# Three layers of gated attention: part of L1's and L2's softmax on GpSimd, another order of steps, and fillers in L2

## The chip, the cores and the metric

The kernel runs as one program on one NeuronCore of a Trainium2 chip. The metric is the device time of that core in microseconds (us). TensorE is called PE in the rows, VectorE DVE, ScalarE ACT, GpSimd POOL, SyncE SP.

## What is computed

The input x is [32, 64, 128] (2,048 tokens of width 128) with a context of [32, 64, 96]. Four layers follow each other; each adds a gated cross attention and a gated feed-forward block:

```python
x = x + tanh(g_xattn[n]) * xattn_n(layernorm(x), ctx)
x = x + tanh(g_ffn[n]) * ffn_n(layernorm(x))
```

The change touches the attentions of layers 1 and 2, "L1" and "L2" below. Both are ordinary multi-head attentions inside each of the 32 batches (64 queries by 64 keys), all in f32:

```python
attn = einsum("bqhd,bkhd->bhqk", Q, K) * scale      # L1: 8 heads of 16; L2: 16 heads of 8
attn = clip(attn, -10000, 10000)                     # L2 alone
attn = softmax(attn); out = einsum("bhqk,bkhd->bqhd", attn, V) @ W_O
```

## The kernel before

The program is written engine by engine: every engine has its own instruction queue in the order of the source, runs it in that order, and waits on semaphores for the others. Nothing but these written orders and waits sets the order of the work.

**Groups and units.** An attention goes through 8 groups of 4 batches (256 tokens), in a loop whose first and last turns are written out. A group has 4 units, u = 0 to 3. A unit is a quarter of the heads for all 4 batches: a score tile of 128 partitions by 256 columns in L1 and by 512 columns in L2. "Unit u+2" means two units on in this order, across the border of a group too.

**A unit's steps**, with the line of the kernel before:

- PE `scores`: query times key into bank u % 2 of PSUM (L1742)
- DVE `scores`: L2 first clamps the tile into SBUF (L833); then the row maximum (L836) and the subtraction (L838), result in SBUF
- ACT `expo`: exponential in place (L1314)
- DVE `weigh`: row sum (L846), reciprocal (L848), product (L850), which raises `prob`
- PE `turn`: waits for `prob`, transposes the tile in blocks of 128 by 128 into bank 2 + u % 2 (L1762). In L1 it first issues 3 "dense" matmuls whose result nobody reads (L1681; 30 ahead of the first unit)
- ACT `probT`: copies the transposed tile to SBUF (L1318)
- PE `values`: waits for that copy, multiplies with V (L1773)
- ACT `narrow`: copies the result out of PSUM, two copies of 32 partitions by 128 columns (L1369)

**Once a group**: PE `value_rows` (L1719) and `queries_keys` (L1691, L1692), ACT copies of values and queries, DVE `keys`, which spreads the keys by head with a mask (L859 in L2, L864 in L1), PE `project_out` (L1803), DVE `add_group` (L886) and two batch norm statistics (L915). GpSimd makes one copy of the context, 96 by 256, for the next group's values (L487), and nothing else during an attention.

**The written orders before**, one group (numbers are units, a prime marks the next group):

```text
PE : value_rows, scores 2, turn 0, project_out, values 0, turn 1, scores 3, queries_keys',
     values 1, turn 2, scores 0', values 2, turn 3, scores 1', values 3
DVE: weigh 1, scores 2, add_group, weigh 2, scores 3, keys', weigh 3, scores 0', weigh 0', scores 1'
ACT: expo 1, values, probT 0, expo 2, narrow 0, probT 1, queries', expo 3, narrow 1, probT 2,
     expo 0', narrow 2, probT 3, narrow 3
```

L3's attention uses the same functions with orders of its own, which stay.

## Time and profile before

| | us |
|---|---|
| median of 3 runs | 1296.91 (1296.06 to 1301.83) |
| the profiled execution, its own time | 1296.64 |
| its span, first to last instruction | 1294.9 |
| L1 attention, first scores to last project_out | 90.8 |
| L2 attention, the same | 165.3 |
| mean granted TensorE clock | 0.802 of full speed |

The two attentions together are about a fifth of the span. A time inside the span is given from its start. The granted clock has two levels, 2.4 GHz (1.00) and 1.2 GHz (0.50); a figure between them is a mean over a stretch.

### The profile page before, as it was taken

The page shows a single profiled execution, that of the slowest core. Times are in us where ns is not written, and L with a number is a line of the kernel's source. Part 1 is how long each engine was busy: PE and PEld are TensorE (multiplying, and loading weights), DVE is VectorE, ACT ScalarE, POOL GpSimd, SP SyncE. Part 2 cuts the span into 40 slices and gives each one's busy share as a digit, 9 for nine tenths or more (in the row PEclk, how much of TensorE's full clock was granted, in tenths as well). Part 3 has the DMA queues.
Part 4 walks back from the last instruction along what each step waited for, and adds up shares of the span by engine and source line. Part 5 has one row for each costly group of instructions (what it writes and reads, how often), then busy time and mean ns, then how long its engine had stood idle before and what let it go on. Part 6 is the DMA issues. An engine that isn't in the chain of part 4 may idle for free.

```text
span 1294.9 us, 22960 instructions
## 1 busy us (share of the span) xinstructions
PE 896.7 (69%) x7815; PEld 721.9 (56%) x7818; DVE 797.8 (62%) x1904; ACT 477.3 (37%) x1085; POOL 233.0 (18%) x280
## 2 busy tenths in 40 slices
PE   0336335048994783889975779993899999739992
PEld 0216122046763772556653679992677777628771
DVE  3864878966885235888776636555766566462334
ACT  0441308114552452344341343331343344205551
POOL 1000000000000671000000047760000000006771
PEclk9756668567995895677586789995999999659996
DMA  7200000006001118000000101118000000001113
GB/s 190 80 1 1 0 1 0 0 1 147 0 1 33 44 49 234 1 1 0 0 1 0 33 27 47 47 42 213 2 2 0 0 0 0 11 27 45 51 51 109
DMA packets 73143, 48.25 MB, mean 37 GB/s; under 512 B 19642, under 2 KB 65732, under 8 KB 73092
## 3 DMA queue, kind: packets, MB, share of 16 engines
q1 hardware_dynamic: 64484, 31.80, 9.2%
q0 software_dynamic: 6656, 13.64, 3.5%
q10 hardware_dynamic: 1952, 2.15, 0.5%
q8 instruction: 30, 0.49, 0.2%
q14 instruction: 21, 0.17, 0.0%
HBM read 33.93 MB, written 13.63 MB: 37 GB/s over the span
## 4 chain that ended last, share of the span: by engine, by line
PE 47%; DVE 27%; POOL 9%; issue 7%; ACT 6%; DMA 2%; DVEq 0%; SPq 0%; another core or an unknown queue 0%; POOLq 0%; ACTq 0%
PE ps L1909 6%; POOL rows_y L499 4%; POOL arena L494 4%; PE ps L1773 3%; PE ps L1742 3%; PE ps L1803 3%; PE ps L1923 3%; PE ps L1498 3%; PE ps L1762 3%; PE ps L1699 2%; PE ps L1709 2%; PE ps L1787 2%; PE ps L1726 2%; PE ps L1751 2%; DVE bst L523 2%
## 5 line engine op out<-in xcount | busy, mean ns | idle before, releaser
L1909 PE MATMUL ps<-arena 128*128 128x128 f32 x1152 | 153.8, 284 | 0.0
L494 POOL DMA_INDIRECT arena<-rows_x,row_in x104 | 102.8, 988 | 276.7 <-DVEq L1116 245.9
L1909 PEld LDWEIGHTS ps<-arena 128*128 128x128 f32 x1152 | 141.4, 197 | 1.4
L499 POOL DMA_INDIRECT rows_y<-arena,row_out x104 | 108.9, 1047 | 56.4 <-issue 21.3
L1923 PE MATMUL ps<-arena 128*128 x832 | 116.1, 283 | 1.4 <-DVE arena L1079 1.3
L1066 DVE COPY arena<-arena 128x644 f32 (+1 forms) x104 | 61.9, 595 | 78.1 <-DVE arena L1079 31.9
L1923 PEld LDWEIGHTS ps<-arena 128*128 128x128 f32 x832 | 102.1, 193 | 6.0 <-issue 3.3
L1498 PE MATMUL ps<-ident,xh 128*128 128x128 f32 x128 | 36.9, 446 | 85.9 <-DVE xh L555 69.8
L1314 ACT ACTIVATE arena<-arena 128x512 f32<-128x512 f32 (+1 forms) x96 | 53.7, 559 | 111.5 <-DVE arena L838 111.2
L1440 ACT ACTIVATE arena<-ps,arena 128x128 f32<-128x128 f32 x256 | 73.2, 368 | 46.9 <-PE ps L1909 46.9
L1773 PE MATMUL ps<-arena 128*64 128x64 f32 x768 | 71.3, 256 | 19.7 <-ACT arena L1318 16.2
L846 DVE TENSOR_REDUCE arena<-arena 128x8 f32<-128x512 f32 (+1 forms) x96 | 57.1, 595 | 44.1 <-ACT arena L1314 42.8
L1773 PEld LDWEIGHTS ps<-arena 128*64 128x64 f32 x768 | 61.7, 166 | 40.2 <-ACT arena L1318 26.3
L1498 PEld LDWEIGHTS ps<-ident,xh 128*128 128x128 f32 x128 | 22.9, 186 | 99.2 <-DVE xh L555 76.0
L1318 ACT COPY arena<-ps 128x512 f32<-128x512 f32 (+1 forms) x96 | 49.4, 514 | 73.1 <-PE ps L1762 69.4
L1742 PE MATMUL ps<-arena 32*64 32x128 f32 (+1 forms) x512 | 67.7, 401 | 9.1 <-DVE arena L859 6.6
L1079 DVE TENSOR_TENSOR arena<-ps,arena 128x128 f32<-128x128 f32 x64 | 18.7, 292 | 85.6 <-PE ps L1923 85.6
L487 POOL COPY arena<-ctxT 96x256 f32 x16 | 6.9, 429 | 331.2 <-PE ps L1726 168.7
L1762 PE MATMUL ps<-ident,arena 128*128 128x128 f32 x320 | 62.5, 317 | 1.6 <-DVE arena L850 1.4
L1901 PE MATMUL ps<-ident,arena 128*128 128x128 f32 x104 | 32.8, 315 | 41.8 <-DMA arena<-rows_x,row_in 41.0
L850 DVE TENSOR_TENSOR arena<-arena 128x512 f32<-128x512 f32 (+1 forms) x96 | 57.9, 603 | 3.5 <-DVE arena L848 0.2
L1657 PE MATMUL ps<-wffT,arena 128*128 128x128 f32 x96 | 13.9, 319 | 54.1 <-DVE arena L774 54.1
(289 smaller groups left out, 1770.2 us busy)
## 6 DMA issues: line engine op xcount, KB each, us to landing
arena<-rows_y SPq DMA_DIRECT2D x20, 256.0 KB, 4.6
arena<-in_L_ffn_w SPq DMA_DIRECT2D x2, 2048.0 KB, 9.5
arena<-in_L_ffn_w SPq DMA_DIRECT2D x16, 256.0 KB, 6.5
rows_x<-xh SPq DMA_DIRECT2D x3, 1024.0 KB, 5.4
rows_x<-zero SPq DMA_DIRECT2D x1, 2560.0 KB, 9.9
arena<-in_L_ffn_gate_proj SPq DMA_DIRECT2D x8, 256.0 KB, 4.9
arena<-in_L_ffn_up_proj SPq DMA_DIRECT2D x8, 256.0 KB, 4.8
arena<-in_L_ffn_down_proj SPq DMA_DIRECT2D x1, 2048.0 KB, 9.9
```

Of the source, the lines that this page charges most:

```text
L494: g.indirect_dma_start(xq[:, q % 4, :], None, rows_x, bass.IndirectOffsetOnAxis(row_in[:, q:q + 1], 0)).then_inc(sem(f"xq_loaded{q % 4}"), 16)
L499: g.indirect_dma_start(rows_y, bass.IndirectOffsetOnAxis(row_out[:, q:q + 1], 0), yq[:, q % 4, :], None).then_inc(sem(f"y_scattered{q % 4} ...
L846: own(v.tensor_reduce(t["sum"][:, u, 0:n], p_, AX.X, ALU.add))
L850: v.tensor_tensor(p_, p_, t["rec"][:, u, 0:n].unsqueeze(2).to_broadcast([P, n, S]), ALU.mult).then_inc(sem("prob"), 1)
L1066: v.tensor_copy(wst[:, s_ % 4, 0:WS[l]].unsqueeze(1), table(l)[:, bass.ds(e, 1), 0:WS[l]]).then_inc(sem("w_staged"), 1)
L1440: s.activation(hT[:, s_ % 2, f, :], ps[:, s_ % 2, P * f:P * f + P], fn, bias=b1[:, f:f + 1]).then_inc(sem("hidden_ready"), 1)
L1498: ins = pe.transpose(ps[0:w, c % 2, P * k:P * k + P], src[:, j, :], ident[:, :])
L1742: ins = pe.matmul(o.rearrange("p (h c s) -> p h c s", c=2, s=S)[:, :, c, :], t["q"][r:r + 32, 0, lo:lo + S], t["k"][r:r + 32, :, lo:lo + S ...
L1762: ins = pe.transpose(ps[:, 2 + u % 2, P * k:P * k + P], t["p"][:, u, P * k:P * k + P], ident[:, :])
L1773: ins = pe.matmul(ps[0:64, 4 + u % 2, S * hh:S * hh + S], t["v"][:, 4 * hh + u, 64 * k:64 * k + 64], t["pt"][:, u % 2, k, S * hh:S * hh + ...
L1909: ins = pe.matmul(ps[:, 2 * m + s_ % 2, P * f:P * f + P], wst[:, s_ % 4, lo:lo + P], xqT[:, s_ % 2, :], start=True, stop=True)
L1923: ins = pe.matmul(ps[:, 4 + s_ % 2, 0:P], hT[:, s_ % 2, f, :], w2[:, P * f:P * f + P], start=(f == 0), stop=(f == NF - 1))
```

## The change

It does five things to the attentions of L1 and L2.

1. GpSimd gets two new steps for each unit: `total` adds the two halves of each row of exponentials (64 columns to 32) into a new tile `half`, and `weigh` does the product with the reciprocal and raises `prob`. DVE keeps `inverse`: it waits for `half`, sums what is left (half as many columns) and takes the reciprocal.
2. L2 clamps the row maximum (128 by 8) instead of the tile; the lower clamp rides with the subtraction, and one more pass over the tile in SBUF takes the minimum with 0.
3. The orders of DVE, ACT and PE are written anew.
4. `values` writes its two halves to partitions 0 to 63 and 64 to 127 and alternates between them; `narrow` makes four copies of 32 by 64 in place of two.
5. The dense matmuls are issued in L2 as well, 3 before each turn and 30 before the first.

The orders after, one group:

```text
PE  : value_rows, scores 2, turn 0, project_out, values 0, scores 3, turn 1, queries_keys',
      values 1, scores 0', turn 2, values 2, scores 1', turn 3, values 3
DVE : scores 2, inverse 0, add_group, scores 3, inverse 1, keys', scores 0', inverse 2,
      scores 1', inverse 3
POOL: total 0, weigh 3 (of the group before), total 1, weigh 0, context copy, total 2, weigh 1,
      total 3, weigh 2
ACT : values, expo 2, probT 0, expo 3, narrow 0, probT 1, queries', narrow 1, expo 0', probT 2,
      expo 1', narrow 2, probT 3, narrow 3
```

Ahead of the first group DVE does keys, scores 0 and scores 1, ACT expo 0 and expo 1, and PE queries_keys, scores 0 and scores 1.

```diff
@@ -384,6 +384,7 @@
             o = 256
             d = {}
             d["q"] = view(o, w // P * GT).rearrange("p (c t) -> p c t", t=GT)
+            d["half"] = view(o + GT, 1024).rearrange("p (u n s) -> p u n s", u=4, s=S // 2)
             o += 2048
             n = 8 if l == 3 else 128 // HEADS[l] and (32 // (P // HEADS[l]))
             d["k"] = view(o, n * GT).rearrange("p (c t) -> p c t", t=GT)
...
+            def weigh_groups(l, src):
+                t = att(l)
+                n = 4 if l == 1 else 8
+                w = n * S
+                g.memset(t["v_all"], 0.0).then_inc(sem("v_cleared"), 1)
+
...
+                def total(i, u):
+                    g.wait_ge(sem("s_exp"), UNITS * i + (UB[l] + u + 1))
+                    p_ = t["p"][:, u, 0:w].rearrange("p (n s) -> p n s", s=S)
+                    g.tensor_tensor(t["half"][:, u, 0:n, :], p_[:, :, 0:S // 2], p_[:, :, S // 2:S], ALU.add
+                                    ).then_inc(sem("half_ready"), 1)
+
+                def weigh(i, u):
+                    g.wait_ge(sem("rec_ready"), UNITS * i + (UB[l] + u + 1))
+                    p_ = t["p"][:, u, 0:w].rearrange("p (n s) -> p n s", s=S)
+                    g.tensor_tensor(p_, p_, t["rec"][:, u, 0:n].unsqueeze(2).to_broadcast([P, n, S]), ALU.mult
+                                    ).then_inc(sem("prob"), 1)
+
+                def group(i, first=False, more=True):
+                    total(i, 0)
+                    if not first:
+                        weigh(i - 1, 3)
+                    total(i, 1)
+                    weigh(i, 0)
+                    if more:
+                        stage_context(i + 1)
+                    total(i, 2)
+                    weigh(i, 1)
+                    total(i, 3)
+                    weigh(i, 2)
+
+                stage_context(0)
+                group(0, first=True)
+                with g.Fori(1, NG - 1) as i:
+                    group(i)
+                group(NG - 1, more=False)
+                weigh(NG - 1, 3)
+
...
                 if last < 2 * l + 2:
                     continue
@@ -818,7 +863,7 @@
                 sub = 4 if l != 1 else 2
                 w = S * sub * 2
                 n_k = 4 if l == 3 else NSUB[l]
-                steps = {"vec_own": UNITS * (4 if l == 2 else 3) + 2, f"k_ready_{l}": n_k, f"s_sub_{l}": UNITS,
+                steps = {"vec_own": UNITS * (2 if l == 1 else 4 if l == 2 else 3) + 2, f"k_ready_{l}": n_k, f"s_sub_{l}": UNITS,
                          f"x_added_{l}": 1}
                 if l == 3:
                     steps["o_half_3"] = 4
@@ -829,14 +874,25 @@
                     s_ = ps[:, u % 2, 0:w].rearrange("p (n s) -> p n s", s=S)
                     p_ = t["p"][:, u, 0:w].rearrange("p (n s) -> p n s", s=S)
                     v.wait_ge(sem("s_mm"), UNITS * i + (UB[l] + u + 1))
+                    own(v.tensor_reduce(t["max"][:, u, 0:n], s_, AX.X, ALU.max))
+                    own.wait()
+                    top = t["max"][:, u, 0:n].unsqueeze(2).to_broadcast([P, n, S])
                     if l == 2:
-                        own(v.tensor_scalar(p_, s_, CLAMP, -CLAMP, ALU.min, ALU.max))
+                        own(v.tensor_scalar(t["max"][:, u, 0:n], t["max"][:, u, 0:n], CLAMP, -CLAMP, ALU.min, ALU.max))
                         own.wait()
-                        s_ = p_
-                    own(v.tensor_reduce(t["max"][:, u, 0:n], s_, AX.X, ALU.max))
-                    own.wait()
-                    own(v.tensor_tensor(p_, s_, t["max"][:, u, 0:n].unsqueeze(2).to_broadcast([P, n, S]),
-                                        ALU.subtract), f"s_sub_{l}")
+                        own(v.scalar_tensor_tensor(p_, s_, -CLAMP, top, ALU.max, ALU.subtract))
+                        own.wait()
+                        own(v.tensor_scalar(p_, p_, 0.0, None, ALU.min), f"s_sub_{l}")
+                        return
+                    own(v.tensor_tensor(p_, s_, top, ALU.subtract), f"s_sub_{l}")
+
+                def inverse(i, u):
+
+                    n = 2 * sub
+                    v.wait_ge(sem("half_ready"), UNITS * i + (UB[l] + u + 1))
+                    own(v.tensor_reduce(t["sum"][:, u, 0:n], t["half"][:, u, 0:n, :], AX.X, ALU.add))
+                    own.wait()
+                    v.reciprocal(t["rec"][:, u, 0:n], t["sum"][:, u, 0:n]).then_inc(sem("rec_ready"), 1)
                 def weigh(i, u):
@@ -889,22 +945,35 @@
                 def group(i, first=False, more=True):
-                    weigh(i, 1)
-                    scores(i, 2)
-                    if not first:
-                        add_group(i - 1)
-                    weigh(i, 2)
-                    scores(i, 3)
-                    if more:
-                        keys(i + 1)
-                    weigh(i, 3)
-                    if l == 3:
+                    if l != 3:
+                        scores(i, 2)
+                        inverse(i, 0)
+                        if not first:
+                            add_group(i - 1)
+                        scores(i, 3)
+                        inverse(i, 1)
+                        if more:
+                            keys(i + 1)
+                            scores(i + 1, 0)
+                        inverse(i, 2)
+                        if more:
+                            scores(i + 1, 1)
+                        inverse(i, 3)
...
@@ -1365,35 +1435,43 @@
                     if l == 3:
                         return
                     s.wait_ge(sem(f"av_mm_{l}"), UNITS * i + (u + 1))
-                    for c in range(2):
-                        ins = s.copy(t["o"][32 * u:32 * u + 32, 0:GT].rearrange("p (h c s) -> p h c s", h=2, c=2)[:, :, c, :],
-                                     ps[32 * c:32 * c + 32, 4 + u % 2, 0:P].rearrange("p (h s) -> p h s", h=2))
+                    for b in range(4):
+                        ins = s.copy(t["o"][32 * u:32 * u + 32, S * b:S * b + S], ps[32 * b:32 * b + 32, 4 + u % 2, 0:S])
                     ins.then_inc(sem(f"o_other_{l}"), 1)
...
@@ -1678,7 +1758,7 @@
                 def dense(bank, n):
                     for _ in range(n):
-                        pe.matmul(ps[:, bank, GT:2 * GT], onesb[:, :], q0[:, 0:GT], start=True, stop=True)
+                        pe.matmul(ps[:, bank, 0:GT], onesb[:, :], q0[:, 0:GT], start=True, stop=True)
                 def queries_keys(i):
@@ -1755,7 +1835,7 @@
                 def turn(i, u):
-                    if l == 1:
+                    if l != 3:
                         dense(2 + u % 2, 30 if isinstance(i, int) and i == u == 0 else 3)
                     pe.wait_ge(sem("prob"), UNITS * i + (UB[l] + u + 1))
                     for k in range(sub):
@@ -1768,9 +1848,9 @@
                         pe.wait_ge(sem(f"o_other_{l}"), UNITS * i + (u + 1))
-                        for hh in range(2):
-                            for k in range(sub):
-                                ins = pe.matmul(ps[0:64, 4 + u % 2, S * hh:S * hh + S],
+                        for k in range(sub):
+                            for hh in range(2):
+                                ins = pe.matmul(ps[64 * hh:64 * hh + 64, 4 + u % 2, 0:S],
                                                 t["v"][:, 4 * hh + u, 64 * k:64 * k + 64],
                                                 t["pt"][:, u % 2, k, S * hh:S * hh + S], start=(k == 0), stop=(k == sub - 1))
                         ins.then_inc(sem(f"av_mm_{l}"), 1)
@@ -1813,6 +1893,21 @@
                     if not first:
                         project_out(i - 1)
                     values(i, 0)
+                    if l != 3:
+                        scores(i, 3)
+                        turn(i, 1)
+                        if more:
+                            queries_keys(i + 1)
+                        values(i, 1)
+                        if more:
+                            scores(i + 1, 0)
+                        turn(i, 2)
+                        values(i, 2)
+                        if more:
+                            scores(i + 1, 1)
+                        turn(i, 3)
+                        values(i, 3)
+                        return
                     turn(i, 1)
                     scores(i, 3)
                     if more:
```

## Rows read from the trace of the kernel before

**Rows 1.** The page, busy time of each engine over the span:

```profile
PE 896.7 (69%) x7815; PEld 721.9 (56%) x7818; DVE 797.8 (62%) x1904; ACT 477.3 (37%) x1085; POOL 233.0 (18%) x280
```

**Rows 2.** Timeline, first and last PE work of the two stages (start, length, us):

```profile
301.19 1.27 PE L1742 MATMUL ps<-arena 32*64 32x128 f32 x16 [1.17 <-DVE arena L864]
...
390.71 1.23 PE L1803 MATMUL ps<-wo,arena 128*128 128x128 f32 x4 [0.61 <-ACT arena L1369]
...
516.84 2.21 PE L1742 MATMUL ps<-arena 32*64 32x256 f32 x16 [1.94 <-DVE arena L859]
...
681.43 0.71 PE L1803 MATMUL ps<-wo,arena 128*128 128x128 f32 x4 [0.61 <-ACT arena L1369]
```

**Rows 3.** Windows: stretch, length, busy time by engine, PEclk, DMA share, GB/s:

```profile
340.00:350.00 10.00, 9.44 (x94) 7.14 (x94) 8.69 (x25) 5.73 (x19) 0.07 (x1) 1.00 0.00 0
...
521.00:529.00 8.00, 4.30 (x24) 2.80 (x25) 6.99 (x10) 2.47 (x5) 0.00 (x0) 0.50 0.00 0
...
553.00:561.00 8.00, 5.95 (x45) 4.32 (x42) 6.69 (x14) 2.38 (x6) 0.00 (x0) 0.71 0.02 3
...
633.00:641.00 8.00, 8.00 (x48) 5.55 (x47) 5.78 (x13) 2.56 (x6) 0.00 (x0) 0.50 0.00 0
```

**Rows 4.** Groups of POOL: line, names, count | busy us, mean ns | idle:

```profile
L487 POOL COPY arena<-ctxnT 96x256 f32 x8 | 3.2, 398 | 74.0 <-PE ps L1719 69.9 <-PEq L1833 4.1
...
L457 POOL CAST identb<-ident 128x128 bf16<-128x128 f32 x1 | 0.3, 291 | 0.1
```

**Rows 5.** Timeline of L1, single steps of the chain of a unit:

```profile
303.54 1.12 PE L1742 MATMUL ps<-arena 32*64 32x128 f32 x8
...
338.84 0.50 PE L1719 MATMUL ps<-wv,arena 96*128 96x128 f32 x3
...
339.51 0.40 POOL L487 COPY arena<-ctxnT 96x256 f32 x1 [10.02 <-PE ps L1719]
...
345.41 0.65 PE L1742 MATMUL ps<-arena 32*64 32x128 f32 x8
...
346.11 0.42 DVE L836 TENSOR_REDUCE arena<-ps 128x4 f32<-128x256 f32 x1
...
346.57 0.42 DVE L838 TENSOR_TENSOR arena<-ps,arena 128x256 f32<-128x256 f32 x1
...
379.69 0.68 PE L1773 MATMUL ps<-arena 128*64 128x64 f32 x8 [0.53 <-ACT arena L1318]
...
388.15 0.38 PE L1762 MATMUL ps<-ident,arena 128*128 128x128 f32 x2
...
388.57 0.37 ACT L1318 COPY arena<-ps 128x256 f32<-128x256 f32 x1
```

**Rows 6.** Timeline of L2, the same steps, and one of L3:

```profile
534.79 1.97 PE L1773 MATMUL ps<-arena 128*64 128x64 f32 x16
...
536.22 1.14 DVE L859 TENSOR_SCALAR arena<-arena,headmask 128x256 f32<-128x256 f32 x4
...
537.74 1.97 PE L1742 MATMUL ps<-arena 32*64 32x256 f32 x8
...
539.76 0.69 DVE L833 TENSOR_SCALAR arena<-ps 128x512 f32<-128x512 f32 x1 [0.75 <-PE ps L1742]
...
541.54 1.12 PE L1762 MATMUL ps<-ident,arena 128*128 128x128 f32 x4
...
542.59 1.08 PE L1742 MATMUL ps<-arena 32*64 32x256 f32 x8
...
543.13 0.59 ACT L1318 COPY arena<-ps 128x512 f32<-128x512 f32 x1
...
543.38 0.20 DVE L848 RECIPROCAL arena<-arena 128x8 f32<-128x8 f32 x1
...
543.77 1.15 PE L1773 MATMUL ps<-arena 128*64 128x64 f32 x16
...
1024.81 1.15 PE L1787 MATMUL ps<-arena 64*64 64x64 f32 x32
```

More of the change, by code:

```diff
@@ L482, in _ @@
                 g.wait_ge(sem("att_open"), l)
[L483 to L487 removed]
+                if l == 3:
+                    with g.Fori(0, NG) as i:
+                        g.wait_ge(sem(f"v_mm_{l}"), 4 * i + 4)
+                        g.tensor_copy(ctxs[:, :], src[:, bass.ds(i * GT, GT)]).then_inc(sem("ctx_staged"), 1)
+                else:
+                    weigh_groups(l, src)
                 if last < 2 * l + 2:
@@ L889, in group @@
                 def group(i, first=False, more=True):
-                    weigh(i, 1)
-                    scores(i, 2)
-                    if not first:
-                        add_group(i - 1)
-                    weigh(i, 2)
-                    scores(i, 3)
-                    if more:
-                        keys(i + 1)
-                    weigh(i, 3)
-                    if l == 3:
-                        outputs(i, 0)
-                    if more:
-                        scores(i + 1, 0)
-                        weigh(i + 1, 0)
-                        scores(i + 1, 1)
-                    if l == 3:
+                    if l != 3:
[12 more added lines that the diff above has]
+                        inverse(i, 3)
+                    else:
+                        weigh(i, 1)
+                        scores(i, 2)
+                        if not first:
+                            add_group(i - 1)
+                        weigh(i, 2)
+                        scores(i, 3)
+                        if more:
+                            keys(i + 1)
+                        weigh(i, 3)
+                        outputs(i, 0)
+                        if more:
+                            scores(i + 1, 0)
+                            weigh(i + 1, 0)
+                            scores(i + 1, 1)
                         outputs(i, 1)
@@ L928, in attention @@
                 scores(0, 0)
-                weigh(0, 0)
+                if l == 3:
+                    weigh(0, 0)
                 scores(0, 1)
@@ L1378, in group @@
                         expo(i, 1)
+                        probT(i, 0)
+                        expo(i, 2)
+                        probT(i, 1)
+                        if more:
+                            queries(i + 1)
+                        expo(i, 3)
+                        probT(i, 2)
+                        outputs(i, 0)
+                        if more:
+                            expo(i + 1, 0)
+                        probT(i, 3)
+                        outputs(i, 1)
+                        return
+                    expo(i, 2)
                     probT(i, 0)
-                    expo(i, 2)
+                    expo(i, 3)
                     narrow(i, 0)
@@ L1384, in group @@
                         queries(i + 1)
-                    expo(i, 3)
                     narrow(i, 1)
-                    probT(i, 2)
-                    if l == 3:
-                        outputs(i, 0)
                     if more:
                         expo(i + 1, 0)
+                    probT(i, 2)
+                    if more:
+                        expo(i + 1, 1)
                     narrow(i, 2)
@@ L1403, in attention @@
                 expo(0, 0)
+                if l != 3:
+                    expo(0, 1)
                 with s.Fori(0, NG - 1) as i:
@@ L1815, in group @@
                     values(i, 0)
+                    if l != 3:
+                        scores(i, 3)
+                        turn(i, 1)
+                        if more:
+                            queries_keys(i + 1)
+                        values(i, 1)
+                        if more:
+                            scores(i + 1, 0)
+                        turn(i, 2)
+                        values(i, 2)
+                        if more:
+                            scores(i + 1, 1)
+                        turn(i, 3)
+                        values(i, 3)
+                        return
                     turn(i, 1)
```

15 lines of the change are left out of this document (5 added, 10 removed).

## The prediction

> **What bounds the kernel now.** The page first: over the span PE is the busiest engine and DVE the next, and neither is full [rows 1], so what matters is how the two attentions run inside. The timeline gives their lengths: L1 from 301.19 to 390.71 + 1.23, 90.8 us, and L2 from 516.84 to 681.43 + 0.71, 165.3 us [rows 2]. For 8 groups of 4 units that is 2.8 us a unit in L1 and 5.2 us in L2. The windows say what fills them. In L1 PE works 9.44 of 10 us at full clock and DVE 8.69: the two run abreast, nearly full. In L2 DVE works about 7 of 8 us and the clock of PE changes sides: at 0.50 PE is busy for all of 633 to 641, at 0.71 it is busy 5.95 of 8 [rows 3]. So both stages are today loose pipelines, in which several units are in flight. That rests on the written orders: PE runs turn u and then scores u+2, DVE runs weigh u ahead of scores u+1, so no turn waits for scores that PE has only just issued.
>
> **What the change takes off.** DVE loses the product of each unit and half of the row sum; GpSimd is idle for 10.02 us between context copies [rows 5] and has the room. That part does what it says. It is the order that decides.
>
> **The new order closes a ring.** Follow one unit. On DVE, inverse u stands behind scores u+2. Scores u+2 on DVE needs PE's scores u+2. PE's turn u waits for the product u on GpSimd, which needs inverse u. And PE's scores u+3 stand in its queue behind turn u and values u, for every u. So:
>
> PE scores u+2, DVE scores u+2, DVE inverse u, GpSimd weigh u, PE turn u, ACT probT u, PE values u, PE scores u+3, and again.
>
> Every step waits for the one before it, and one turn of the ring moves the kernel on by one unit. The stage's length becomes the number of turns times the ring's latency, whatever the engines' busy times are. Only expo, total, add_group, narrow and the dense matmuls lie beside the ring (total u+1 runs on GpSimd right behind weigh u-1, long before it is wanted). Narrow with four copies instead of two costs ACT more, but ACT then waits for most of each turn, so I price it at nothing; so too the bank columns of the dense matmuls.
>
> **The ring in L1, PE at the lower clock** (first row of each kind; a handoff between engines is 0.05, as from 345.41 + 0.65 to 346.11, and 0.17 to GpSimd, as from 338.84 + 0.50 to 339.51 [rows 5]):
> - PE scores 1.12 + 0.05; maximum to subtraction 0.46; subtraction 0.42 [rows 5]. Together 2.05.
> - Half row sum: 256 columns take 0.42 [rows 5] and 512 take 0.69 [rows 6], so 128 take 0.29; its wait 0.04; reciprocal at most 0.20 [rows 6], I take 0.18. Then 0.17 to GpSimd. Together 0.68.
> - GpSimd product, 256 columns. No row shows a product on this engine. A copy of 128 columns takes 0.291 and one of 256 takes 0.398 [rows 4]: 0.184 fixed and 0.84 ns for each column read. Below: the price of the copy, 0.40. Above: two copies, 0.80. A product reads two operands, so I take 0.184 + 512 x 0.84 ns = 0.61, and 0.05 to PE.
> - Transposes 0.38 at full clock [rows 5]; scores went from 0.65 to 1.12, a factor of 1.7, so 0.65; 0.05; ACT 0.37 [rows 5]; 0.05. Together 1.12.
> - Values. Before, 8 records took 0.68 at full clock [rows 5]. After, neighbours write different halves of the partitions. Above: the old price, 1.17 at the lower clock. Below: the rate of L3's small tiles, 32 records in 1.15 [rows 6], 8 in 0.29, 0.50 at the lower clock. I take 0.80.
>
> Sum 5.3 us, against 2.8 us a unit now.
>
> **The ring in L2, lower clock**: scores 1.97 + 0.05; maximum 0.69 + 0.04; clamp of 128 by 8, like the reciprocal, 0.20 + 0.04; subtraction 0.69; minimum over 512 columns in SBUF between 0.42 (L859 does 256 in 1.14 / 4 = 0.285) and 0.69, taken 0.42; half row sum 0.42 + 0.04; reciprocal 0.20; 0.17; product 0.184 + 1024 x 0.84 ns = 1.04 (bounds 0.62 and 1.6); 0.05; transposes 1.12; 0.05; ACT 0.59; 0.05; values between 1.0 and 1.97, taken 1.40 [rows 4, 6]. Sum 9.2 us, against 5.2. Clamping the maximum instead of the tile buys nothing here: the old clamp's 0.69 is gone and 0.24 + 0.42 comes.
>
> **Once a group** the ring also holds value_rows (0.5 at full clock [rows 5], 0.9 at half), and queries_keys with the keys: PE about 2.0 (as a scores step at the lower clock), an ACT copy 0.59, DVE 1.14 [rows 6], which together outlast the ACT copy and values that run beside them (about 2.2) by some 1.4. That is 2.3 us a group.
>
> **The PE clock.** PE's share of work falls: at full clock scores, dense, transposes and values are about 2 of 4.3 us in L1. The one stretch in which PE works with such gaps, 4.30 of 8 us, ran at 0.50 throughout, and even 5.95 of 8 brought the clock down to 0.71; fully busy PE at 0.50 stayed there from 633 to 641 [rows 3]. So I take the lower clock for both stages. The dense matmuls in L2 work against it, but three of them a turn can't fill the wait of one ring.
>
> **The sum.** 30 turns of the ring in each stage (32 units less the two ahead of the loop), 7 group extras, and the ends (the first scores as before; the 30 dense matmuls; the last two units without scores; last project_out), which I set at 11 us in L1 and 17 in L2, where DVE also adds its offset to x.
> - L1: 30 x 5.3 + 7 x 2.3 + 11 = 186, less 90.8: +95 us.
> - L2: 30 x 9.2 + 7 x 2.3 + 17 = 309, less 165.3: +144 us.
>
> Together +239. The groups that follow the 30 dense matmuls may still see full clock; I take off 7. Against the profiled execution (span 1294.9, own time 1296.6) that is a span of 1527 and a time of 1529; the median of the runs, 1296.9, is 0.3 above it. Prediction: 1530 us.
>
> **Two rules of the Trainium skill.** The price of the product has only neighbours in the trace [rows 4]. The Trainium skill's GPSIMD Engine Reference, section 3.1, measures an f32 tensor_tensor of 2,048 columns at 4,497 ns, an estimate of 0.56 and 1.12 us here; by it the sum would be 1 us higher. SBUF — State Buffer of the Trainium skill, "Who interferes with whom", says that a DVE instruction in a two-port mode and a GpSimd one lock each other out for a whole instruction. That speaks against the change in L2; it is the third rival.
>
> **Rivals.**
> - *The ring at full clock* (the dense matmuls hold PE up, as 30 of them did in L1). The PE terms shrink to 0.70, 0.38 and 0.48 in L1, sum 4.3, and to 1.13, 0.65 and 0.85 in L2, sum 7.3 [rows 5, 6]; extras 1.4, ends 9 and 15. L1 148, L2 244: +136, 1433 us. A mixture of the two clocks lies between. For it: L1 ran at 1.00 for 80 us. Against: it did so with PE 94% busy [rows 3]. Chance 0.27, mixtures below 1490 included.
> - *The pipeline survives, faster than before.* If product u were raised before PE reaches turn u, the busiest engine would set the pace: L1 about 9.4 us a group (PE, unchanged), L2 about 14.5 (four times scores 1.08, transposes 0.65, values 1.15 and dense 0.4, and 1.5 once), for 8 groups 75 + 116 + ends of 15: about 50 less, 1247 us. It decides only if a turn of the ring costs less than 2.35 us in L1 and 3.6 in L2; even DVE scores, inverse and GpSimd's product alone come to some 2.2 and 3.9. Chance 0.04.
> - *GpSimd and DVE lock each other out.* If both new GpSimd steps of a unit held up a DVE step by their length (0.4 to 1.04 us), the ring would grow by about 0.8 in 60 turns: +48, 1578 us. Against: in the ring the two rarely run at once. The rule would act so; no row shows GpSimd at work beside L859. Chance 0.06.
> - *The change does nothing measurable*: the loss of order and the gain of DVE cancel. No mechanism makes them meet. Chance 0.01.
>
> **How the numbers follow.** The ring at the lower clock has 0.62; its own range, with the bounds of GpSimd's product (-19 to +22), values (-21 to +28) and the minimum (+8), which won't all fall on one side, is 1490 to 1575. For 8 in 10 the range has to reach into the full-clock case: 1430 to 1575. Under 0.5% is about what a measurement of this kernel can't tell from no change. Faster 0.04, same 0.01, slower 0.95.
>
> **What would show it.** In the profile after: PE, DVE, ACT and POOL all idle for most of a unit in both stages; POOL's product released by DVE's reciprocal, PE's transposes by POOL, ACT's copy by PE, in the chain that ended last; a unit of about 5.3 and 9.2 us (4.3 and 7.3 at full clock); granted clock near 0.5 in both. DVE's busy time falls although the span grows, and nothing else in the kernel moves. It is wrong if transposes find their product done, if scores u+3 start on PE before turn u, or if GpSimd's product takes far over 1.6 us.

## The result, and the profile after

| | before | after |
|---|---|---|
| median | 1297.41 us (4 runs, 1296.06 to 1301.83) | 1511.55 us (4 runs, 1510.78 to 1513.59) |
| ratio, 95% interval | | 1.161 (1.157 to 1.166) |
| span of the profiled execution | 1294.9 | 1511.8 |
| L1 attention, first scores to last project_out | 90.8 | 181.9 |
| L2 attention, the same | 165.3 | 294.3 |
| granted clock over the span | 0.80 | 0.71 |

The change makes the kernel 16% slower. The prediction said 1530 us and slower at 0.95. The two attentions grew by 91.1 and 129.0 us, together 220; the span grew by 217. All of it is in the two stages: in front of them, between them and behind them nothing moves by more than 5 us.

The page of the changed kernel, busy times and the granted clock in 40 slices (beside [rows 1]):

```profile
PE 989.0 (65%) x7940; PEld 757.5 (50%) x7941; DVE 747.1 (49%) x1872; ACT 497.6 (33%) x1213; POOL 321.1 (21%) x408
...
PEclk9566585655555696555555555799969999956997
```

DVE does 51 us less than before and POOL 88 more, as the change intends; PE's 92 more are almost all in the two stages (L1 84.0 to 129.7, L2 142.8 to 181.4), where its granted clock is lower and L2 has the new dense matmuls. Now one unit of L1, in the timeline (start, length, in brackets the idle time ahead and who ended it), from PE's scores to the end of its values:

```profile
454.81 1.12 PE L1822 MATMUL ps<-arena 32*64 32x128 f32 x8
...
455.97 0.42 DVE L877 TENSOR_REDUCE arena<-ps 128x4 f32<-128x256 f32 x1 [3.69 <-PE ps L1822]
456.43 0.42 DVE L887 TENSOR_TENSOR arena<-ps,arena 128x256 f32<-128x256 f32 x1
456.77 0.28 DVE L893 TENSOR_REDUCE arena<-arena 128x4 f32<-128x128 f32 x1
...
457.08 0.18 DVE L895 RECIPROCAL arena<-arena 128x4 f32<-128x4 f32 x1
...
457.34 0.61 POOL L498 TENSOR_TENSOR arena<-arena 128x256 f32<-128x256 f32 x1 [3.95 <-DVE arena L895]
...
458.01 0.69 PE L1842 MATMUL ps<-ident,arena 128*128 128x128 f32 x2 [1.33 <-POOL arena L498]
458.73 0.37 ACT L1388 COPY arena<-ps 128x256 f32<-128x256 f32 x1 [0.56 <-PE ps L1842]
...
459.16 0.69 PE L1853 MATMUL ps<-arena 128*64 128x64 f32 x8 [0.46 <-ACT arena L1388]
...
459.78 1.22 PE L1799 MATMUL ps<-wv,arena 96*128 96x128 f32 x4
```

Read it downwards: each row starts when the one above has ended, or nearly. PE's scores of one unit start at 454.81 and the next work behind the unit's values at 459.78, 4.97 us later. DVE had waited 3.69 us for these scores, POOL 3.95 us for the reciprocal, PE 1.33 us for the product with its dense matmuls already behind it. The same ring in L2:

```profile
704.46 1.97 PE L1822 MATMUL ps<-arena 32*64 32x256 f32 x8 [0.78 <-DVE arena L915]
...
706.46 0.69 DVE L877 TENSOR_REDUCE arena<-ps 128x8 f32<-128x512 f32 x1 [2.15 <-PE ps L1822]
707.19 0.17 DVE L881 TENSOR_SCALAR arena<-arena 128x8 f32<-128x8 f32 x1
707.39 0.69 DVE L883 SCALAR_TENSOR_TENSOR arena<-ps,arena 128x512 f32<-128x512 f32 x1
708.12 0.43 DVE L885 TENSOR_SCALAR arena<-arena 128x512 f32<-128x512 f32 x1
708.46 0.41 DVE L893 TENSOR_REDUCE arena<-arena 128x8 f32<-128x256 f32 x1
...
708.91 0.20 DVE L895 RECIPROCAL arena<-arena 128x8 f32<-128x8 f32 x1
709.19 1.04 POOL L498 TENSOR_TENSOR arena<-arena 128x512 f32<-128x512 f32 x1 [8.75 <-DVE arena L895]
...
710.29 1.12 PE L1842 MATMUL ps<-ident,arena 128*128 128x128 f32 x4 [3.11 <-POOL arena L498]
711.44 0.59 ACT L1388 COPY arena<-ps 128x512 f32<-128x512 f32 x1 [2.23 <-PE ps L1842]
...
712.08 1.12 PE L1853 MATMUL ps<-arena 128*64 128x64 f32 x16 [0.68 <-ACT arena L1388]
...
713.13 1.97 PE L1822 MATMUL ps<-arena 32*64 32x256 f32 x8
```

From scores to scores 8.67 us (704.46 to 713.13). PE waits 3.11 us for POOL. Of the waits over the whole span (who waited for whom: total, times, longest) these three are the ring's:

```profile
POOL arena L498 <- DVE arena L895: 353.3, 60, 9.0
...
PE ps L1842 <- POOL arena L498: 130.7, 58, 3.6
...
ACT arena L1388 <- PE ps L1842: 143.7, 87, 4.6
```

The first came up nowhere before; it is the new link. The windows (as in [rows 3]) give the clock of a piece of each stage:

```profile
385.00:425.00 40.00, 28.85 (x170) 18.77 (x171) 11.34 (x36) 12.92 (x48) 7.88 (x16) 0.50 0.00 0
...
700.00:780.00 80.00, 49.69 (x300) 30.69 (x301) 25.41 (x66) 21.73 (x63) 14.98 (x19) 0.52 0.00 0
```

PE works 28.9 of 40 us in L1 and 49.7 of 80 in L2 and sits at its lower level, 1.2 GHz, nearly throughout.

### The profile page after: what moved, and what is told of

Read it like the earlier page. It is cut to its first block, busy times and chain, and to the rows that moved or that the text cites. A ratio compares the mean times of both kernels' runs of the same rounds, so it can differ in the third digit from the quotient of the medians.

```text
span 1511.8 us, 23486 instructions
## 1 busy us (share of the span) xinstructions
PE 989.0 (65%) x7940; PEld 757.5 (50%) x7941; DVE 747.1 (49%) x1872; ACT 497.6 (33%) x1213; POOL 321.1 (21%) x408
## 4 chain that ended last, share of the span: by engine, by line
PE 34%; issue 26%; DVE 21%; POOL 12%; ACT 4%; DMA 3%; ACTq 0%; DVEq 0%; POOLq 0%; SPq 0%
PE ps L2004 5%; POOL rows_y L544 4%; POOL arena L539 4%; PE ps L2018 3%; PE ps L1578 2%; PE ps L1883 2%; PE ps L1779 2%; POOL arena L498 2%; PE ps L1789 2%; POOL arena L492 2%; PE ps L1867 2%; PE ps L1806 2%; PE ps L1842 2%; PE ps L1831 2%; DVE bst L568 2%
## 5 line engine op out<-in xcount | busy, mean ns | idle before, releaser
L1842 PE MATMUL ps<-ident,arena 128*128 128x128 f32 x320 | 77.9, 375 | 133.2 <-POOL arena L498 130.7
L877 DVE TENSOR_REDUCE arena<-ps 128x8 f32<-128x512 f32 (+1 forms) x96 | 57.6, 600 | 210.2 <-PE ps L1822 204.5
L498 POOL TENSOR_TENSOR arena<-arena 128x256 f32<-128x256 f32 (+1 forms) x64 | 53.0, 828 | 353.3 <-DVE arena L895 353.3
L1842 PEld LDWEIGHTS ps<-ident,arena 128*128 128x128 f32 x320 | 46.0, 184 | 162.7 <-POOL arena L498 159.0
L1822 PE MATMUL ps<-arena 32*64 32x128 f32 (+1 forms) x512 | 92.4, 518 | 12.9 <-DVE arena L915 7.5
L1853 PE MATMUL ps<-arena 128*64 128x64 f32 x768 | 57.5, 320 | 20.6 <-ACT arena L1388 19.3
L1853 PEld LDWEIGHTS ps<-arena 128*64 128x64 f32 x768 | 45.7, 217 | 46.8 <-ACT arena L1388 33.1
L1822 PEld LDWEIGHTS ps<-arena 32*64 32x64 f32 x512 | 46.2, 209 | 34.2 <-issue 30.2
L1439 ACT COPY arena<-ps 32x64 f32<-32x64 f32 x256 | 51.8, 202 | 34.7 <-PE ps L1853 32.1
L1996 PE MATMUL ps<-ident,arena 128*128 128x128 f32 x104 | 32.8, 315 | 41.1 <-DMA arena<-rows_x,row_in 40.3
```

What stands on the lines that cost most here:

```text
L498: g.tensor_tensor(p_, p_, t["rec"][:, u, 0:n].unsqueeze(2).to_broadcast([P, n, S]), ALU.mult).then_inc(sem("prob"), 1)
L877: own(v.tensor_reduce(t["max"][:, u, 0:n], s_, AX.X, ALU.max))
L1822: ins = pe.matmul(o.rearrange("p (h c s) -> p h c s", c=2, s=S)[:, :, c, :], t["q"][r:r + 32, 0, lo:lo + S], t["k"][r:r + 32, :, lo:lo + S ...
L1842: ins = pe.transpose(ps[:, 2 + u % 2, P * k:P * k + P], t["p"][:, u, P * k:P * k + P], ident[:, :])
L1853: ins = pe.matmul(ps[64 * hh:64 * hh + 64, 4 + u % 2, 0:S], t["v"][:, 4 * hh + u, 64 * k:64 * k + 64], t["pt"][:, u % 2, k, S * hh:S * hh ...
```

## The experiments

Each run also gave its profile; L1 and L2 are read from it as in the table above, the clock from a window over the stage. A stage's length thus comes from one execution. It lies within 6 us of its kernel's median, except for run 5 (1301.7, the shortest of 1301.7, 1314.0, 1329.5 and 1331.3) and run 12 (1287.9, the shortest of ten). "Old values" always goes with the old narrow. "Before" on the same chips had medians of 1298 to 1301 us.

| run | median us | ratio to before | L1 us, clock | L2 us, clock |
|---|---|---|---|---|
| before | 1297.4 | | 90.8, 0.95 | 165.3, 0.71 |
| after | 1511.6 | 1.161 | 181.9, 0.52 | 294.3, 0.53 |
| 1 after, no GpSimd steps | 1509.7 | 1.161 (1.156 to 1.167) | 178.8, 0.52 | 290.1, 0.53 |
| 2 after, DVE order opened | 1415.0 | 1.089 (1.083 to 1.094) | 143.2, 0.57 | 233.0, 0.55 |
| 3 and ACT order opened | 1358.4 | 1.043 (1.039 to 1.048) | 132.9, 0.55 | 193.0, 0.58 |
| 4 after, 12 fillers | 1451.9 | 1.117 (1.112 to 1.122) | 149.0, 0.93 | 268.1, 0.71 |
| 5 as 3, 8 fillers | 1321.7 | 1.020 (1.012 to 1.028) | 107.7, 0.96 | 167.1, 0.84 |
| 6 before, values halves | 1323.5 | 1.018 (1.013 to 1.023) | 113.3, 0.70 | 165.9, 0.54 |
| 7 before, fillers in L2 | 1300.9 | 1.001 (0.998 to 1.004) | 93.2, 0.92 | 171.4, 0.74 |
| 8 before, clamp, halves, fillers | 1313.2 | 1.010 (1.007 to 1.013) | 113.3, 0.70 | 158.8, 0.75 |
| 9 as 3, old values | 1340.1 | 1.028 (1.021 to 1.036) | 110.3, 0.82 | 195.2, 0.66 |
| 10 as 9, 6 fillers | 1320.3 | 1.019 (1.012 to 1.026) | 105.8, 0.96 | 175.4, 0.82 |
| 11 after, old values | 1533.8 | 1.181 (1.173 to 1.189) | 189.4, 0.55 | 310.8, 0.54 |
| 12 before, clamp | 1295.3 | 0.996 (0.994 to 0.999) | 90.7, 0.96 | 158.2, 0.76 |

**Run 1: is it the order or GpSimd?** The old weigh takes the place of inverse; GpSimd keeps only the context copy.

```diff
                 def inverse(i, u):
-                    v.wait_ge(sem("half_ready"), UNITS * i + (UB[l] + u + 1))
...
-                    v.reciprocal(t["rec"][:, u, 0:n], t["sum"][:, u, 0:n]).then_inc(sem("rec_ready"), 1)
+                    weigh(i, u)
```

> The changed kernel with GpSimd's two steps taken back: where DVE ran inverse u it now runs the old weigh u (whole row sum, reciprocal, product); all written orders stay. If the ring of waits is the cause, GpSimd is only one link of it: the link costs 0.19 us less in L1 (0.42 + 0.04 + 0.18 + 0.04 + 0.42 + 0.05 for 0.29 + 0.04 + 0.18 + 0.17 + 0.61 + 0.05) and 0.21 less in L2, times 30 turns each: 12 us off, about 1500 us. If work on GpSimd is the cause, the time falls back to about 1300.

1509.7 us. With no work on GpSimd but the context copy the kernel is as slow as with it. The link made the stages 3.1 and 4.2 us shorter, against 12 us worked out for both, and of that 2 us are left in the median; the rest of the ring is unchanged. So the loss does not come from the work on GpSimd. What is left are the orders and the three other parts; runs 2 and 3 test the first, runs 6, 7, 8 and 12 the others.

**Run 2: open the ring at DVE.** Only DVE's order changes: inverse u goes ahead of scores u+2.

```diff
-                        scores(i, 2)
                         inverse(i, 0)
+                        scores(i, 2)
                         if not first:
                             add_group(i - 1)
-                        scores(i, 3)
                         inverse(i, 1)
+                        scores(i, 3)
...
```

> The changed kernel with one order changed: DVE runs inverse u ahead of scores u+2 instead of behind it. The ring through inverse and GpSimd opens. A second, shorter ring is left, because ACT runs expo u+2 ahead of probT u: PE scores, DVE scores, ACT expo, ACT probT, PE values. At the lower clock it is 1.17 + 0.93 + 0.42 + 0.37 + 0.05 + 0.63 = 3.6 us in L1 and 2.02 + 2.22 + 0.63 + 0.59 + 0.05 + 1.05 = 6.6 us in L2, so about 50 and 65 us less: near 1395 us, down to 1330 if PE gets its full clock back. If GpSimd's own steps are the cost wherever they stand, the time stays near 1510.

1415.0 us: 97 us back for an edit that adds and removes no instruction, with GpSimd's steps untouched. It was worked out at 1395: L1 at 132 and is 143, L2 at 229 and is 233. The timeline of this run in L1 shows the second ring:

```profile
343.98 1.12 PE L1823 MATMUL ps<-arena 32*64 32x128 f32 x8 [0.43 <-DVE arena L920]
...
345.60 0.42 DVE L887 TENSOR_TENSOR arena<-ps,arena 128x256 f32<-128x256 f32 x1
345.65 0.63 PE L1843 MATMUL ps<-ident,arena 128*128 128x128 f32 x2
...
346.06 0.42 ACT L1385 ACTIVATE arena<-arena 128x256 f32<-128x256 f32 x1 [1.61 <-DVE arena L887]
...
346.50 0.37 ACT L1389 COPY arena<-ps 128x256 f32<-128x256 f32 x1
...
346.92 0.70 PE L1854 MATMUL ps<-arena 128*64 128x64 f32 x8 [0.64 <-ACT arena L1389]
...
347.55 1.12 PE L1823 MATMUL ps<-arena 32*64 32x128 f32 x8
...
350.07 0.84 ACT L1440 COPY arena<-ps 32x64 f32<-32x64 f32 x4
...
351.36 0.70 PE L1854 MATMUL ps<-arena 128*64 128x64 f32 x8 [1.52 <-ACT arena L1389]
```

The transposes of unit u end at 346.28, but ACT first does expo u+2 (346.06), which had to wait for this unit's DVE scores; only then it copies the transposed tile (346.50), and PE's values and next scores come behind it. From scores to scores (343.98 to 347.55) that is 3.57 us, where 3.6 had been worked out. In the next turn ACT also does narrow (350.07) between expo and the copy, 0.84 us that the expectation had left out, and PE waits 1.52 us for the copy.

**Run 3: open ACT's order too.**

```diff
-                    expo(i, 2)
                     probT(i, 0)
+                    expo(i, 2)
...
```

> As the run before, and ACT runs probT u ahead of expo u+2 too, so no order closes a ring of one unit. What is left is a ring over two units (about 5.0 us for two in L1, 9 in L2 at the lower clock), and then the busiest engine sets the pace, PE about 9.4 to 10.4 us a group in L1, PE and DVE about 14.5 to 18 in L2. The ring theory gives 1250 to 1290 us, faster than the kernel before; the theory that GpSimd's steps themselves cost gives a time well above 1300.

1358.4 us: faster by 57 again, so the second ring was real; but a miss by some 90 us against what I expected, and slower than before. The window over L1:

```profile
300.00:420.00 120.00, 108.98 (x719) 77.35 (x716) 50.29 (x155) 51.67 (x197) 34.50 (x68) 0.56 0.05 8
```

PE is busy 109 of 120 us at a clock of 0.56. PE works nearly without a break, at about half its speed. The kernel before did the same kind of work at 1.00 [rows 3].

**Run 4: the clock alone, ring closed.**

```diff
-                        dense(2 + u % 2, 30 if isinstance(i, int) and i == u == 0 else 3)
+                        dense(2 + u % 2, 30 if isinstance(i, int) and i == u == 0 else 12)
```

> The changed kernel with 12 dense matmuls ahead of each turn instead of 3, in L1 and L2. It tests the clock alone. If more fillers bring PE to its full clock, the ring shrinks from 5.3 to about 4.3 us and from 9 to about 7.2, some 88 us in all: 1424 us, granted clock near 1.0 in both stages. If the clock stays at 0.5, the 12 take 2.6 us, 0.4 more than PE waits in L1, and the time is about 1524.

```profile
296.00:445.00 149.00, 116.83 (x1070) 84.52 (x1070) 51.91 (x163) 59.55 (x216) 35.17 (x71) 0.93 0.08 16
570.00:838.00 268.00, 194.97 (x1389) 127.33 (x1390) 97.19 (x242) 75.56 (x223) 58.97 (x71) 0.71 0.00 0
```

L1 at 0.93 takes 149.0 us, where the full-clock rival had worked out 148. L2 came only to 0.71 and to 268.1, between its two cases (244 and 309). The run was expected at 1424 us and took 1452, mostly because L2 did not reach the full clock (24 us above the full-clock case). In L1 the lower clock is worth 33 us (181.9 to 149.0); the prediction's two cases, 186 and 148, had put 38 on it.

**Run 5: opened orders and 8 fillers.**

```diff
-                        dense(2 + u % 2, 30 if isinstance(i, int) and i == u == 0 else 3)
+                        dense(2 + u % 2, 30 if isinstance(i, int) and i == u == 0 else 8)
```

> The kernel of the third run (both orders opened) with 8 dense matmuls ahead of each turn instead of 3. There PE was busy for 120 of 133 us in L1 and 166 of 193 in L2 at a clock of 0.55 and 0.58: the ring is gone and PE at its lower clock is the bound. If that is so, and more fillers lift the clock as 12 of them did for the changed kernel in L1 (0.52 to 0.93), L1 falls from 133 to about 95 us and L2 from 193 to about 150: 1275 us. If a hidden wait sets the pace, the clock may rise and the time stays near 1358; if the clock stays low, 5 more fillers of 0.2 us cost 1 us a unit: about 1410.

1321.7 us, 37 less than run 3 with more work in it: PE at its lower clock was the bound in run 3. The four times spread over 30 us, but the longest (1331.3) is still shorter than the shortest of run 3 (1352.3). Whether this kernel is slower than before is less sure: its two shorter times have their middle at 1307.8. The 1275 expected did not come; PE is busy for 93.3 of the 107.7 us of L1, which is taken up at run 10.

**Runs 6, 7 and 8: the other parts on the kernel before.** Run 6 has part 4 alone (values in two halves, narrow in four copies), run 7 part 5 alone, run 8 both and the clamp. The edit of run 6:

```diff
-                        for hh in range(2):
-                            for k in range(sub):
-                                ins = pe.matmul(ps[0:64, 4 + u % 2, S * hh:S * hh + S],
+                        for k in range(sub):
+                            for hh in range(2):
+                                ins = pe.matmul(ps[64 * hh:64 * hh + 64, 4 + u % 2, 0:S],
...
-                    for c in range(2):
...
+                    for b in range(4):
+                        ins = s.copy(t["o"][32 * u:32 * u + 32, S * b:S * b + S], ps[32 * b:32 * b + 32, 4 + u % 2, 0:S])
```

> The kernel before with the fourth part of the change alone: values alternate between two halves of the partitions, and narrow makes four copies. In the changed kernel 16 records of values in L2 took 1.12 us at the lower clock against 1.97 before. L1 runs on DVE and gains nothing; in L2 PE is the bound for about half of the time: 0.85 x 32 x 0.5 = 14 us, 1287 us. The theory that only the order cost anything says same or faster; slower would mean that this part has a cost of its own, such as less PE activity and a lower clock.

1323.5 us, 1.8% slower, where 1287 was expected. Windows over L1 and L2:

```profile
304.00:417.00 113.00, 101.48 (x791) 73.40 (x791) 69.95 (x195) 59.19 (x216) 2.78 (x7) 0.70 0.11 21
544.00:710.00 166.00, 148.68 (x988) 95.66 (x988) 131.00 (x243) 77.08 (x223) 2.79 (x7) 0.54 0.00 0
```

L1 went from 90.8 to 113.3 us and its clock from 0.95 to 0.70, with no order of steps changed. The records of values are shorter, as intended (0.45 for 8 at full clock, where before they took 0.68), and the stage is longer. The rows where the clock first falls, about 320 us into run 6, with the same place of the kernel before:

```profile
318.81 0.85 ACT L1369 COPY arena<-ps 32x64 f32<-32x64 f32 x4
...
320.11 0.70 PE L1772 MATMUL ps<-arena 128*64 128x64 f32 x8 [1.13 <-ACT arena L1318]
```

```profile
316.21 0.52 ACT L1369 COPY arena<-ps 32x128 f32<-32x128 f32 x2
...
317.18 0.68 PE L1773 MATMUL ps<-arena 128*64 128x64 f32 x8 [0.56 <-ACT arena L1318]
```

Here PE waits 1.13 us in place of 0.56, and the records that follow are those of the lower clock. Of the 0.57 us more, 0.33 are narrow's: its four copies take 0.85 us and its two took 0.52, and ACT's copy of the transposed tile stands behind them. The rest fits the shorter values (0.23). The run changes both at once, so it does not show which of them the clock follows.

The edit of run 7; run 8 has the edits of runs 6, 7 and 12:

```diff
-                        pe.matmul(ps[:, bank, GT:2 * GT], onesb[:, :], q0[:, 0:GT], start=True, stop=True)
+                        pe.matmul(ps[:, bank, 0:GT], onesb[:, :], q0[:, 0:GT], start=True, stop=True)
...
-                    if l == 1:
+                    if l != 3:
                         dense(2 + u % 2, 30 if isinstance(i, int) and i == u == 0 else 3)
```

> The kernel before with the fifth part alone: dense matmuls ahead of each turn in L2 as in L1. L2's granted clock rises from 0.71 to near 1.0 and its pace is set by DVE, 16.9 us of work a group: about 150 us instead of 165, 1282 us. If the fillers only add PE time and the clock does not rise, 32 x 0.6 us: 1316.

1300.9 us, where 1282 was expected: no change that can be measured. Three fillers a turn hardly lift L2's clock here (0.71 to 0.74).

> The kernel before with the clamp on the maximum, the values halves and the fillers in L2, and its own orders, no work on GpSimd. If nothing but the orders costs in the change, this is the faster of all so far: 1275 us. If one of the three parts costs, it is slower than the best of the two runs before it.

1313.2 us. It is not the fastest; L1 shows the loss of run 6 to the tenth (113.3). In L2 the clock is 0.75, against 0.54 in run 6, and the stage 7 us shorter, so there the fillers, or the clamp, give back what part 4 takes. Parts 2, 4 and 5 together cost the kernel before about 15 us, of the 214 that the whole change costs.

**Runs 9 and 10: opened orders with the old values and narrow**, with 3 and with 6 fillers. Against run 3:

```diff
-                        for k in range(sub):
-                            for hh in range(2):
-                                ins = pe.matmul(ps[64 * hh:64 * hh + 64, 4 + u % 2, 0:S],
+                        for hh in range(2):
+                            for k in range(sub):
+                                ins = pe.matmul(ps[0:64, 4 + u % 2, S * hh:S * hh + S],
...
-                        dense(2 + u % 2, 30 if isinstance(i, int) and i == u == 0 else 3)
+                        dense(2 + u % 2, 30 if isinstance(i, int) and i == u == 0 else 6)
```

(the last two lines in run 10 alone, and narrow as it was before in both).

> The kernel of the third run (both orders opened, GpSimd at work) with the values and narrow of before: one half of the partitions, two copies. The halves alone cost the kernel before 22 us in L1, where the clock fell from 0.95 to 0.70. If the halves also keep the opened kernel at its lower clock, this one returns to about 1.0 in L1: PE needs 9.4 to 10 us a group, L1 80 to 90 us, and L2 about 145: 1265 us. If the clock stays low without them, values cost 0.4 us a unit more in L1 and 0.85 in L2: about 1395 us.

> As the run before, with 6 dense matmuls ahead of each turn instead of 3. If the clock holds anyway, they cost 0.32 us a unit in both stages, 20 us more than the run before. If 3 were too few to hold it, this one is the faster: 1275 to 1290.

1340.1 and 1320.3 us. The old values bring L1's clock from 0.55 to 0.82, 6 fillers to 0.96; neither reaches its expectation (1265, and 1275 to 1290). Near full clock L1 still takes 105.8 us, 15 more than before, with this window and these rows from run 10:

```profile
310.00:400.00 90.00, 78.76 (x781) 61.09 (x780) 48.22 (x150) 42.63 (x138) 33.29 (x65) 1.00 0.00 0
```

```profile
351.54 0.38 PE L1844 MATMUL ps<-ident,arena 128*128 128x128 f32 x2
351.95 0.37 ACT L1389 COPY arena<-ps 128x256 f32<-128x256 f32 x1 [1.04 <-PE ps L1844]
...
352.38 0.68 PE L1855 MATMUL ps<-arena 128*64 128x64 f32 x8 [0.46 <-ACT arena L1389]
```

DVE has work for only 48 of 90 us: what the change wanted from DVE is there. But PE waits 0.46 us between the transposes of a unit and its values for ACT's copy, in about two of the four units of a group: the new PE order puts values 2 and 3 right behind turns 2 and 3, where scores 0' and 1' stood between them before, and the copy ran beside those for the most part. The waits of PE over the whole of L1, first in run 10, then in the kernel before:

```profile
PE ps L1855 <- ACT arena L1389: 7.8, 17, 0.5
PE ps L1824 <- DVE arena L920: 4.5, 8, 1.2
```

```profile
PE ps L1773 <- ACT arena L1318: 5.4, 9, 1.2
```

So the wait for the copy is 2.4 us longer than before and the wait for the keys (L920) 3.3 us; before, that one was 1.2 us. They are the smaller part of the 15 us. PE's own work grew by more: it was busy for 84.0 us of L1 and is busy for 93.4 in run 10, and the three more fillers of each unit alone are 10 us (six take 0.83 us, three 0.50). Run 5 has the same 7.8 us of waiting and 93.3 us of work. This also says what the change could win in L1 at best: PE was busy for 84.0 of 90.8 us there and DVE for 70, so at that clock taking work off DVE had some 7 us to gain, an estimate from these three numbers.

**Run 11: the values term of the closed ring.** The edit of run 9, made on the changed kernel with its orders as they are:

```diff
-                                ins = pe.matmul(ps[64 * hh:64 * hh + 64, 4 + u % 2, 0:S],
+                                ins = pe.matmul(ps[0:64, 4 + u % 2, S * hh:S * hh + S],
```

> The changed kernel, ring closed, with the values and narrow of before. It tests the values term of the ring. At the lower clock the step from values to the next scores grows from 0.63 to about 1.0 us in L1 and from 1.05 to 1.90 in L2: 30 x (0.37 + 0.85) = 37 us more, 1548 us. If the longer values step lifts the clock instead, the time falls below 1511.

1533.8 us, 22 more than after; 37 were worked out. The values step does lie on the ring. The clock stays low in both stages (0.55 and 0.54), so in the closed ring it is not part 4 that holds it down.

**Run 12: the clamp alone, on the kernel before.**

```diff
-                    if l == 2:
-                        own(v.tensor_scalar(p_, s_, CLAMP, -CLAMP, ALU.min, ALU.max))
...
+                    if l == 2:
+                        own(v.tensor_scalar(t["max"][:, u, 0:n], t["max"][:, u, 0:n], CLAMP, -CLAMP, ALU.min, ALU.max))
+                        own.wait()
+                        own(v.scalar_tensor_tensor(p_, s_, -CLAMP, top, ALU.max, ALU.subtract))
+                        own.wait()
+                        own(v.tensor_scalar(p_, p_, 0.0, None, ALU.min), f"s_sub_{l}")
```

> The kernel before with the second part alone, the clamp on the maximum. On DVE a unit of L2 scores goes from 2.13 us to 0.78 + 0.21 + 0.73 + 0.34 = 2.06: 32 x 0.07 = 2 us less at most, no change that can be measured. The theory that only order and clock matter says 1297.

1295.3 us, ratio 0.996 (0.994 to 0.999): at the edge of what can be told from none, and the lowest median of all. Its L2 is 158.2 us, 7 less than before where 2 had been worked out, but in the shortest of its ten executions; run 8, with the same clamp, has 158.8. Where these 7 us come from was not looked into.

## Why the prediction was right

**The ring.** It holds in its marks but one. The trace shows the steps one behind the other with the waits named; the number of turns times the latency gives the stage; run 1 keeps it with no GpSimd in it; run 2 opens it with one order. The sign that failed is that PE would be idle for most of a unit: it is busy for 71% of L1 and 62% of L2, since at the lower clock its steps and fillers are long; DVE, ACT and POOL are idle for most of it.

**Its size.** The prediction's steps against what was measured, at the lower clock:

| step | L1 said / is | L2 said / is |
|---|---|---|
| scores to DVE's start | 1.17 / 1.16 | 2.02 / 2.00 |
| DVE scores | 0.88 / 0.80 | 2.08 / 2.00 |
| half sum, reciprocal, to POOL | 0.68 / 0.57 | 0.83 / 0.73 |
| product, to PE | 0.66 / 0.67 | 1.09 / 1.10 |
| transposes to values | 1.12 / 1.15 | 1.81 / 1.79 |
| values to the next scores | 0.80 / 0.62 | 1.40 / 1.05 |
| one turn | 5.3 / 4.97 | 9.2 / 8.67 |

(Is: starts of the rows above, as 456.77 - 455.97 = 0.80.) The largest misses are the values, priced too high between their bounds; they explain 0.18 of 0.33 and 0.35 of 0.56 us. The handoff from DVE to GpSimd, taken at 0.17, is 0.08 (457.08 + 0.18 to 457.34). Groups were worked out at 4 x 5.3 + 2.3 = 23.5 us in L1; context copies on POOL at 348.77 and 371.82 are 23.05 apart. So the once-a-group extras are 3.2 instead of 2.3, which gives part of it back. Of these 0.9 us, 0.3 are value_rows: the row read for it, 338.84, has three of its four matmuls; four take 1.22 at the lower clock (459.78), not 0.9. The stages came to 181.9 for 186 and 294.3 for 309. The misses of single steps partly cancel, and the 18 us between 1530 and 1511.6 are mostly L2's.

**GpSimd's price.** L498 is the product, L492 the half sum, from the groups of L2 (count | busy, mean ns):

```profile
L498 POOL TENSOR_TENSOR arena<-arena 128x512 f32<-128x512 f32 x32 | 33.3, 1043 | 219.6 <-DVE arena L895 219.6
...
L492 POOL TENSOR_TENSOR arena<-arena 128x256 f32<-128x256 f32 x32 | 24.8, 774 | 11.3 <-ACT arena L1384 11.3
```

The product of 512 columns takes 1.043 us; worked out from one column read at a time it was 1.04, and 0.61 in L1, where it is 0.61 too. By the figure of the Trainium skill's GPSIMD Engine Reference, section 3.1, the estimates had been 1.12 and 0.56; the rows are nearer to the count of columns read. That the price came out to the hundredth is partly luck. Its two neighbours were not alike (L457 is a cast to bf16, L487 a copy of f32), and the same reckoning misses the half sum: 0.61 for 512 columns read, where L492 takes 0.73 in all turns but one, and 0.40 for 256, where it takes 0.46 in L1.

**The clock.** Taken at the lower level in both stages: it was 0.52 and 0.53. Run 4 shows what the other case costs: with 9 more fillers a turn it lands at 1452 us, between the two clocks, in the range that the prediction had given to their mixture.

**The rivals.** The full-clock ring did not happen in the change; in run 4 it did in L1. The pipeline that survives did not happen; even with both orders open the median stays above the kernel before (runs 3, 5, 9 and 10), so its 1247 us asked for more than an open ring. The lock between GpSimd and DVE does not show in the ring: L885 takes 0.43 us and L498 1.04 throughout.

**What it did not see.** The prediction read DVE's load from single windows. Over the stages DVE works 70 of 91 us in L1 and 131 of 165 in L2, less than its 8.69 of 10 and "about 7 of 8 us"; the forecast does not hang on this. It let the new values order count only as a shorter step. Run 6 shows that part 4, with a narrow that the prediction priced at nothing, costs the kernel before 22 us in L1, and that the clock falls with it. And when the ring is open, PE's own work with the fillers that its clock takes is the bound of L1 (runs 5 and 10), with its waits for ACT's copy and for the keys behind it. Neither changes the result here, since the ring holds everything; both decide what is left when it is opened. Why the clock falls in run 6 is argued, not shown: the rows show shorter PE work, a longer narrow, a longer wait of PE and a lower clock after it. The new values and the new narrow were not taken apart. The PE order of before together with GpSimd's steps and the opened DVE and ACT orders was not run.

## What to carry to other kernels

When work is handed on from engine to engine, write the queues side by side and follow one unit through them: if a step of unit u stands behind a step of unit u+2 on one engine, and the other way round on another, the stage runs as long as the latency of the ring, and the busy times say nothing. An order is checked in all queues it crosses: here opening DVE's gave 97 us and ACT's 57 more. Then ask which engine bounds the stage once it flows: in L1 it was PE, and work taken off DVE could win some 7 us at most. A change that shortens PE's steps or lengthens its waits can leave the stage longer, by way of the clock (run 6); read the granted clock before and after.

## What the runs showed of the hardware

- With the values on alternating halves 16 records take 1.12 us instead of 1.97 at the lower clock. With that and a narrow of four copies, L1 of the kernel before fell from 0.95 to 0.70 and got 22.5 us longer (run 6); its clock first fell after a wait of PE of 1.13 us where it had been 0.56.
- PE that is busy for 109 of 120 us may stay near the lower level (run 3, 0.56), while the same stage with 5 more matmuls of 128 by 256 in bf16 for each unit ran at 0.96 (run 5) and 25 us shorter.
- DVE held GpSimd up once, outside the ring. Timeline of the changed kernel at the opening of L2:

```profile
609.90 0.72 POOL L492 TENSOR_TENSOR arena<-arena 128x256 f32<-128x256 f32 x1 [9.96 <-ACT arena L1384]
...
611.25 2.29 DVE L1003 TENSOR_TENSOR x<-x,offset 128x2048 f32<-128x2048 f32 x1
...
611.96 2.16 POOL L492 TENSOR_TENSOR arena<-arena 128x256 f32<-128x256 f32 x1 [1.34 <-ACT arena L1384]
```

The half sum takes 0.72 us alone and 2.16 while DVE adds two SBUF tensors (L1003, 611.25 to 613.54); it ends 0.6 us after DVE does. The DVE addition is not longer for it: it takes 2.29 us in the kernel before too, with GpSimd idle. SBUF — State Buffer of the Trainium skill, "Who interferes with whom", says that a DVE instruction with two SBUF inputs contends with a GpSimd one that reads SBUF; the trace agrees.
